# Deriving the second norm's statistics from the first's, and casting six first parts on ScalarE

## The chip, the cores and the metric

The kernel runs on one core of one Trainium2 chip. The metric is the device time of one execution in microseconds. Three runs of the kernel before took 723.16, 723.86 and 724.17 us; the median is 723.86.

## What is computed

The input x has 4 batches of 512 tokens with 128 channels. The reference, cut to what matters here:

```python
xn = _layernorm(x)                      # (x - m) / sqrt(v + 1e-5)
x = x + attn0(xn) + block(xn)           # block: h = _ln(xn, g1, b1); causal attention on h;
                                        # a = o @ Wo + bo + xn; h2 = _ln(a, g2, b2); top-2 experts
xn = _layernorm(x)
x = x + attn1(xn) + moe(xn)             # full attention, 8 experts, top 2
```

`attn0` and the attention in `block` are causal, `attn1` is not; each has 16 heads of 8 channels. `block` begins with a second norm of what is normed already. With mean m and variance v of x, the normed xn has mean 0 and variance v/(v + e), so its norm is (x - m) times (v(1 + e) + e²) to the power of -1/2, with e = 1e-5.

## The kernel before, in words

The tokens of a batch lie as 4 tiles of 128 tokens. "u" counts three attentions: 0 is `attn0`, 1 is the one in `block`, 2 is `attn1`. The twelve pairs (batch, u) are worked through in the order of `ATTENTIONS` (line 48). Each attention has 4 quads of 4 heads, and for each quad TensorE computes the scores twice: once for the row maxima ("max", line 896, which VectorE reduces at line 548) and once, transposed, for the exponentials ("scores", line 923, which ScalarE evaluates at line 791). GpSimd zeroes the part above the diagonal (line 1093), and TensorE multiplies by the values (line 944).

Queries and keys are fp32, but the scores' products run in bf16. Therefore each is split into three bf16 parts. A projection ("project", line 864) leaves queries (k = 0) or keys (k = 1) in a PSUM bank. VectorE casts them to the first part (line 499, or line 495 with a bias for u = 1) and subtracts it from the bank to get the remainder (lines 513 and 508). ScalarE casts the remainder to the second part ("second", line 772), GpSimd subtracts for the third ("parts", line 1062). DMAs then lay the parts into a stack for the products (`fill_piece`, line 385). For the first two attentions ScalarE and GpSimd issue a part of these DMAs themselves, SyncE issues all others. The maxima are split likewise by GpSimd, transposed by TensorE, copied to maxT by VectorE (line 558) and laid into the stack by a DMA (line 1217), for which the scores of the quad wait.

A norm is made of three steps. "stats": VectorE takes BN_STATS of the 4 tiles (line 442), aggregates (line 446) and adds epsilon (line 449). GpSimd raises the result to the power of -1/2 (line 1054). "norm": VectorE subtracts and multiplies (line 461). "turn": TensorE transposes the result. The four norms of a batch are x, h (of the normed x), a and y; x and h share one set of small buffers, a and y the other.

The order is written out by hand as a string of letters (`SCORE`, line 101): each letter is the next step of one chain of steps, and the digit behind it is the PSUM bank that the step takes (a digit names the first of two banks where a step takes two; there are 7 banks to take). `plan` (line 125) turns the string into one list of 1363 steps, and every engine walks through that list and does its own share of each step in that order. So an engine that waits in one step holds up all its later steps. `Order` (line 163) works out from the list which step used a bank before and which count of a semaphore stands for it. The chain "A" (`front`) has the norms and projections of a batch; in batches whose second attention comes first (1, 2 and 3), the steps of u = 1 stand before those of u = 0. VectorE, ScalarE and GpSimd each have one counting semaphore for most results (`vector_done`, `scalar_done`, `gpsimd_done`).

The parts that the change and the prediction touch are the "stats" and "norm" steps of h and x, the "project" steps of VectorE, the steps "second" and "scores" of ScalarE, and the "norm" step of GpSimd (line 1051).

## Time and profile before

| what | value |
|---|---|
| median of three runs | 723.86 us |
| the profiled execution | 722.89 us |
| its span, first to last instruction | 721.1 us |
| mean granted TensorE clock | 0.985 |
| TensorE busy | 686.5 us (95%) |
| VectorE busy | 571.8 us (79%), 1127 instructions |
| ScalarE busy | 527.9 us (73%), 645 instructions |
| GpSimd busy | 194.1 us (27%), 461 instructions |
| VectorE's row maxima, line 548 | 344.5 us in 320 instructions |
| ScalarE's exponentials, line 791 | 288.2 us in 320 instructions |

TensorE is busy for nearly the whole span, so most of what the other engines do is hidden beside it. What counts is where TensorE stands idle, and what it waits for there.

### The profile page before, as it was taken

How to read it: one execution, taken by the hardware profiler on the slowest of the kernel's cores; microseconds unless marked ns; L12 is line 12 of the kernel's file. 1: busy time of each engine (PE TensorE's matmuls, PEld its weight loads, DVE VectorE, ACT ScalarE, POOL GpSimd, SP SyncE). 2: the span in 40 equal slices, each digit the busy share in tenths (PEclk: the TensorE clock that was granted, in tenths of full speed). 3: DMA queues.
4: the chain of work that ended last, by engine and by line, in shares of the span. 5: the costliest groups of instructions: out<-in, count | busy, mean ns of one | idle time of the engine just before them, and what ended most of it. 6: DMA issues, size and time to landing. Idle time of an engine off the chain costs nothing.

```text
span 721.1 us, 27651 instructions
## 1 busy us (share of the span) xinstructions
PE 686.5 (95%) x12078; PEld 344.1 (48%) x12078; DVE 571.8 (79%) x1127; ACT 527.9 (73%) x645; POOL 194.1 (27%) x461
## 2 busy tenths in 40 slices
PE   5688999999999999999999999999999999999996
PEld 2333344665744545544444246556454565533234
DVE  5899999365696888889999777766887667699965
ACT  7167777777777687877879976786878556787892
POOL 5165546112341111313543000123362001020010
PEclk9599999999999999999999999999999999999999
DMA  6140464201130120113132200030040000030001
GB/s 155 36 106 16 125 200 127 72 5 65 36 89 13 34 80 3 36 36 87 52 102 71 63 5 22 4 107 13 23 133 17 4 5 21 28 91 13 28 26 41
DMA packets 42151, 39.52 MB, mean 55 GB/s; under 512 B 14360, under 2 KB 37328, under 8 KB 41808
## 3 DMA queue, kind: packets, MB, share of 16 engines
q1 hardware_dynamic: 40688, 36.20, 17.8%
q8 instruction: 95, 1.56, 0.9%
q10 hardware_dynamic: 1152, 1.05, 0.6%
q0 software_dynamic: 192, 0.52, 0.3%
q14 instruction: 24, 0.20, 0.1%
HBM read 10.47 MB, written 1.44 MB: 17 GB/s over the span
## 4 chain that ended last, share of the span: by engine, by line
PE 78%; DVE 10%; ACT 5%; DMA 2%; issue 2%; SPq 2%; POOL 1%; ACTq 0%; POOLq 0%; DVEq 0%
PE psum L845 44%; PE psum L944 15%; PE psum L923 9%; PE psum L896 8%; DVE neg_max L548 6%; ACT probs L791 2%; SPq L395 2%; PE psum L901 1%; ACT k_stack L729 1%; DMA q_stack<-part 1%; PE psum L861 1%; ACT probs L815 1%; DVE acc L703 1%; DMA heads_inv<-inverses 1%; DMA q_stack<-maxT 1%
## 5 line engine op out<-in xcount | busy, mean ns | idle before, releaser
L548 DVE TENSOR_REDUCE neg_max<-psum 128x2 f32<-128x1024 f32 (+2 forms) x320 | 344.5, 1111 | 57.4 <-PE psum L901 31.1
L791 ACT ACTIVATE probs<-psum 128x1024 f32<-128x1024 f32 (+1 forms) x320 | 288.2, 939 | 108.2 <-PE psum L923 106.2
L944 PE MATMUL psum<-probs,v_ones 128*32 128x512 f32 (+3 forms) x1536 | 158.0, 494 | 0.0
L815 ACT ACTIVATE probs<-psum,col 128x512 f32<-128x512 f32 x160 | 100.8, 686 | 57.7 <-PE psum L845 57.3
L896 PE MATMUL psum<-k_stack,q_stack 64*128 64x512 bf16 (+3 forms) x768 | 114.9, 333 | 17.1 <-DMA q_stack<-part 9.3
L1093 POOL TENSOR_SCALAR_AFFINE_SELECT probs<-probs 128x512 f32<-128x512 f32 x128 | 81.0, 639 | 177.0 <-ACT probs L791 161.5
L845 PE MATMUL psum<-ew,probs 128*32 128x128 f32 x4096 | 124.4, 274 | 0.0
L845 PEld LDWEIGHTS psum<-ew,probs 128*32 128x32 f32 x4096 | 109.7, 110 | 18.8 <-issue 17.1
L845 PE MATMUL psum<-normed_T_a,ew 128*32 128x512 f32 x1024 | 117.1, 593 | 0.8 <-DVE neg_max L548 0.7
L923 PE MATMUL psum<-q_stack,k_stack 64*128 64x512 bf16 (+3 forms) x768 | 110.7, 329 | 5.2 <-DVE neg_max L548 2.4
L743 ACT ACT_TABLE_LOAD x76 | 97.5, 1283 | 1.3
L703 DVE SCALAR_TENSOR_TENSOR acc<-psum,gate,acc 128x128 f32<-128x128 f32 x256 | 72.0, 343 | 19.7 <-PE psum L845 18.0
L1079 POOL CAST max_part<-neg_max 128x16 bf16<-128x16 f32 x48 | 9.5, 198 | 250.8 <-DVE neg_max L548 249.2
L896 PEld LDWEIGHTS psum<-k_stack,q_stack 64*128 64x128 bf16 x768 | 36.9, 95 | 83.8 <-issue 27.8
L923 PEld LDWEIGHTS psum<-q_stack,k_stack 64*128 64x128 bf16 x768 | 32.0, 94 | 80.7 <-issue 26.2
L845 PEld LDWEIGHTS psum<-normed_T_a,ew 128*32 128x32 f32 x1024 | 33.3, 110 | 58.2 <-issue 50.3
L944 PEld LDWEIGHTS psum<-probs,v_ones 128*32 128x32 f32 x1536 | 36.4, 108 | 41.9 <-issue 31.2
L901 PEld LDWEIGHTS psum<-above,pick 64*128 64x128 bf16 x1024 | 45.9, 97 | 16.4 <-issue 1.4
L901 PE MATMUL psum<-above,pick 64*128 64x64 bf16 x1024 | 52.9, 194 | 0.0
L845 PE MATMUL psum<-wout,probs 128*32 128x128 f32 x1024 | 33.7, 275 | 0.1
L1062 POOL TENSOR_TENSOR part<-rest,part 128x512 bf16<-128x512 f32 x24 | 27.7, 1172 | 13.4 <-ACT part L772 13.4
L845 PEld LDWEIGHTS psum<-wout,probs 128*32 128x32 f32 x1024 | 26.7, 110 | 8.4 <-issue 5.2
(132 smaller groups left out, 476.7 us busy)
## 6 DMA issues: line engine op xcount, KB each, us to landing
q_stack<-part SPq DMA_DIRECT2D x66, 128.0 KB, 2.5
k_stack<-part SPq DMA_DIRECT2D x66, 128.0 KB, 2.5
heads_raw<-head_sums SPq DMA_DIRECT2D x24, 128.0 KB
heads_inv<-inverses SPq DMA_DIRECT2D x12, 256.0 KB, 3.4
ew<-w_expert_in SPq DMA_DIRECT2D x4, 512.0 KB, 4.5
ew<-w_expert_out SPq DMA_DIRECT2D x4, 512.0 KB, 5.4
q_stack<-k_stack SPq DMA_DIRECT2D x14, 128.0 KB, 2.3
q_stack<-maxT SPq DMA_DIRECT2D x48, 32.0 KB, 1.9
```

What stands on the lines that cost most here:

```text
L548: eng.tensor_reduce(neg_max[:, q % 2, :, xs[0]:xs[-1] + 1, i], src, AX_X, ALU.max, negate=True).then_inc(vector_done.sem, 1)
L703: eng.scalar_tensor_tensor(out=acc_of[b % 2][:, t, :], in0=src[:, t * P:(t + 1) * P], scalar=gate_of[layer][:, t, expert:expert + 1], in1= ...
L743: eng.preload_act_table(table)
L791: eng.activation(dst, src, ACT.Exp, scale=SCALE).then_inc(probs_ready.sem, 1)
L815: ins = eng.activation(probs[:, order.slot[step[:-1]], 2 * k + f, :], two_banks(step)[:, f, :], ACT.Gelu_apprx_tanh if layer else ACT.Gelu ...
L845: ins = eng.matmul(dst[some, :], kept[:, some], moving, start=start, stop=stop)
L896: ins = eng.matmul(dst[:, a, col0:col0 + keys], q_stack[slot][rows_of, head, i * P:(i + 1) * P], k_stack[slot][rows_of, head, 0:keys], sta ...
L901: ins = eng.matmul(dst[:, a, col0:col0 + HALF], pick[rows_of, upper, :], above[rows_of, upper, :], start=False, stop=upper == 1)
L923: ins = eng.matmul(dst[:, a, n * width:(n + 1) * width], k_stack[slot][rows_of, head, j * P:(j + 1) * P], q_stack[slot][rows_of, head, TIL ...
L944: ins = eng.matmul(sum_bank[32 * c:32 * c + V_COLS, q0:TILES * P], v_ones[u][:, j, g // 2 * QH + c, col0:col0 + V_COLS], probs[:, order.sl ...
L1062: eng.tensor_tensor(part[:, k, 2, :], rest[:, k, :], part[:, k, 1, :], ALU.subtract).then_inc(gpsimd_done.sem, 1)
L1093: eng.affine_select(out=diagonal, in_=diagonal, compare_op=ALU.is_ge, fill=no_chance, base=0, pattern=[[0, QH], [1, P]], channel_multiplie ...
```

## The change

1. The step "stats" of h is dropped (4 of 1363 steps, one for each batch). In "stats" of x VectorE makes two values from the same variance: v + e for the first norm, and v(1 + e) + e² for the second. GpSimd's pow then takes both at once, 8 columns instead of 4, and the pow for h is dropped. The norm of h reads x and its mean instead of the normed x, and the second half of the pow's result.
2. For three attentions, (batch 0, u = 1), (batch 1, u = 1) and (batch 1, u = 0), the first parts of queries and keys are cast by ScalarE, at the place of the "project" step in its own order: an ACTIVATE of Identity with a bias for u = 1, of Copy for u = 0. VectorE waits for it and then subtracts as before.
3. The next batch's x may be loaded only when the norm of h has been made too, and GpSimd's pow of x waits for the norm of h of the batch before.
4. The order of the remaining 1359 steps is the same, but 543 of the 920 steps that take a bank have another bank number. Most of that is a renaming: in 36 steps the step that used the bank before is another one than it was.

The diff, without the string of the order:

```diff
+CAST_BY_SCALAR = ((0, 1), (1, 1), (1, 0))
...
-                  ("second", b, 0, 1), ("parts", b, 0), ("stats", b, "h"), ("norm", b, "h"), ("project", b, 0, 2),
+                  ("second", b, 0, 1), ("parts", b, 0), ("norm", b, "h"), ("project", b, 0, 2),
...
-            if kind in ("second", "gate_exp") or kind == "values" and step[3] % 2 == 1 and step[4] == TILES - 1 or \
+            if kind in ("second", "gate_exp") or kind == "project" and step[3] < 2 and step[1:3] in CAST_BY_SCALAR or kind == "values" and step[3] % 2 == 1 and step[4] == TILES - 1 or \
...
-            if kind in ("norm", "bias", "parts"):
+            if kind in ("bias", "parts") or kind == "norm" and step[2] != "h":
...
-        minus_half = sb("minus_half", [P, TILES])
+        minus_half = sb("minus_half", [P, 2, TILES])
...
-        var_eps_of = [sb(f"var_eps{n}", [P, TILES]) for n in range(2)]
-        rstd_of = [sb(f"rstd{n}", [P, TILES]) for n in range(2)]
+        var_eps_of = [sb(f"var_eps{n}", [P, 2 - n, TILES]) for n in range(2)]
+        rstd_of = [sb(f"rstd{n}", [P, 2 - n, TILES]) for n in range(2)]
...
+            if part_of == 0 and (b, u) in CAST_BY_SCALAR:
+                return scalar_done.sem, order.act["project", b, u, side]
...
-                    eng.tensor_scalar(var_eps[:, :], mean_var[:, :, 1], EPS, None, ALU.add)\
+                    if what == "x":
+                        eng.tensor_scalar(var_eps[:, 1, :], mean_var[:, :, 1], 1.0 + EPS, EPS * EPS, ALU.mult, ALU.add)\
+                           .then_inc(vector_done.sem, 1)
+                        vector_done.count()
+                    eng.tensor_scalar(var_eps[:, 0, :], mean_var[:, :, 1], EPS, None, ALU.add)\
                        .then_inc(vector_done.sem, 1)
...
-                    src = {"x": x_in, "h": normed["x"], "a": a_sum, "y": acc_of[b % 2]}[what]
+                    src = {"x": x_in, "h": x_in, "a": a_sum, "y": acc_of[b % 2]}[what]
...
-                    eng.wait_ge(gpsimd_done.sem, order.pool[step])
+                    eng.wait_ge(gpsimd_done.sem, order.pool["norm", b, "x" if what == "h" else what])
                     for t in range(TILES):
                         eng.tensor_scalar(normed[what][:, t, :], src[:, t, :], mean_var_of[n_set][:, t, 0:1],
-                                          rstd_of[n_set][:, t:t + 1], ALU.subtract, ALU.mult)\
+                                          rstd_of[n_set][:, int(what == "h"), t:t + 1], ALU.subtract, ALU.mult)\
                            .then_inc(vector_done.sem, 1)
...
-                    if u == 1:
-                        eng.tensor_scalar(part[:, k, 0, :], src, bias_qk[:, k:k + 1], None, ALU.add)\
-                           .then_inc(vector_done.sem, 1)
-                        n = vector_done.count()
+                    if (b, u) in CAST_BY_SCALAR:
+                        eng.wait_ge(scalar_done.sem, order.act[step])
                     else:
...
+                if kind == "project" and step in order.act:
+                    u, k = step[2:]
+                    part = part_of_attention(b, u)
+                    eng.wait_ge(work_full.sem, order.work[step] + 1)
+                    if u == 1:
+                        eng.activation(part[:, k, 0, :], one_bank(step), ACT.Identity, bias=bias_qk[:, k:k + 1])\
+                           .then_inc(scalar_done.sem, 1)
+                    else:
+                        eng.activation(part[:, k, 0, :], one_bank(step), ACT.Copy).then_inc(scalar_done.sem, 1)
+                    assert scalar_done.count() == order.act[step]
+                elif kind == "second":
...
-                elif kind == "norm":
+                elif kind == "norm" and step[2] != "h":
...
-                    eng.tensor_tensor(rstd_of[n_set][:, :], var_eps_of[n_set][:, :], minus_half[:, :], ALU.pow)\
+                    if n_set == 0 and b > 0:
+                        eng.wait_ge(vector_done.sem, order.dve["norm", b - 1, "h"])
+                    eng.tensor_tensor(rstd_of[n_set][:, :, :], var_eps_of[n_set][:, :, :], minus_half[:, 0:2 - n_set, :], ALU.pow)\
                        .then_inc(gpsimd_done.sem, 1)
...
-                        eng.wait_ge(vector_done.sem, order.dve["norm", b - 1, "x"])
+                        eng.wait_ge(vector_done.sem, max(order.dve["norm", b - 1, "x"], order.dve["norm", b - 1, "h"]))
```

## Rows read from the trace of the kernel before

**Rows 1.** Busy time by stretch; columns: stretch, length, PE, PEld, DVE, ACT, POOL, clock, DMA

```profile
21.00:60.00 39.00, 32.17 (x446) 14.95 (x442) 36.64 (x52) 18.55 (x25) 16.75 (x42) 0.80 0.23 59
60.00:130.00 70.00, 65.60 (x1004) 28.91 (x1002) 64.11 (x111) 50.87 (x65) 37.92 (x77) 1.00 0.41 120
130.00:330.00 200.00, 198.95 (x3955) 111.53 (x3948) 150.22 (x327) 150.41 (x177) 44.08 (x102) 1.00 0.16 46
```

**Rows 2.** Groups by line, busy us and mean ns; the first from one tile's view

```profile
L442 DVE BATCH_NORM_STATS2 stats<-normed_x x16: 271/275/284, 13.1 to 305.6; 128x6 f32<-128x128 f32 x16
...
L1054 POOL TENSOR_TENSOR rstd<-var_eps,minus_half 128x4 f32<-128x4 f32 x16 | 16.3, 1018 | 36.1 <-DVE var_eps L449 27.2 <-PE psum L845 8.7
...
L1081 POOL TENSOR_TENSOR max_rest<-neg_max,max_part 128x16 f32<-128x16 f32 x48 | 10.5, 219 | 4.0
...
L495 DVE TENSOR_SCALAR part<-psum,bias_qk 128x512 bf16<-128x512 f32 x8 | 6.0, 745 | 1.6 <-PE psum L845 1.6
...
L815 ACT ACTIVATE probs<-psum,col 128x512 f32<-128x512 f32 x160 | 100.8, 686 | 57.7 <-PE psum L845 57.3
...
L799 ACT ACTIVATE head_sums<-psum 128x512 f32<-128x512 f32 x24 | 14.4, 600 | 7.7 <-PE psum L944 7.6
...
L743 ACT ACT_TABLE_LOAD x76 | 97.5, 1283 | 1.3
```

**Rows 3.** Timeline of the start; start us, us, engine, idle before and releaser in brackets

```profile
6.50 1.14 DVE L461 TENSOR_SCALAR normed_x<-x_in,mean_var,rstd 128x128 f32<-128x128 f32 x4 [1.21 <-POOL rstd L1054]
...
8.39 3.60 ACT L729 ACTIVATE k_stack<-one_row 128x4096 bf16<-128x4096 bf16 x1
...
11.13 0.69 DVE L513 TENSOR_TENSOR rest<-psum,part 128x512 f32<-128x512 f32 x1
...
20.81 0.29 PE L896 MATMUL psum<-k_stack,q_stack 64*128 64x128 bf16 x2 [8.32 <-DMA q_stack<-part]
```

**Rows 4.** Timeline at the norms of batch 1

```profile
60.23 1.04 POOL L1054 TENSOR_TENSOR rstd<-var_eps,minus_half 128x4 f32<-128x4 f32 x1
...
61.46 1.76 DVE L461 TENSOR_SCALAR normed_x<-x_in,mean_var,rstd 128x128 f32<-128x128 f32 x4
...
64.01 0.86 DVE L442 BATCH_NORM_STATS2 stats<-normed_x 128x6 f32<-128x128 f32 x4
...
65.40 0.29 DVE L558 CAST maxT<-psum 128x128 bf16<-128x128 f32 x1
...
64.15 0.39 PE L896 MATMUL psum<-k_stack,q_stack 64*128 64x512 bf16 x2 [0.46 <-DVE neg_max L548]
...
69.38 0.39 PE L923 MATMUL psum<-q_stack,k_stack 64*128 64x512 bf16 x2 [1.01 <-DMA q_stack<-maxT]
```

**Rows 5.** Timeline at the projections of batch 0, u = 1

```profile
36.02 1.72 ACT L791 ACTIVATE probs<-psum 128x1024 f32<-128x1024 f32 x2 [1.39 <-PE psum L923]
...
38.51 0.75 DVE L508 SCALAR_TENSOR_TENSOR rest<-psum,bias_qk,part 128x512 f32<-128x512 f32 x1
```

**Rows 6.** Timeline at the projections of batch 1, u = 1

```profile
72.22 1.06 PE L845 MATMUL psum<-normed_T_h,proj_qk 128*32 128x512 f32 x8
...
73.66 1.51 ACT L791 ACTIVATE probs<-psum 128x768 f32<-128x768 f32 x2 [1.09 <-PE psum L923]
...
75.61 0.75 DVE L508 SCALAR_TENSOR_TENSOR rest<-psum,bias_qk,part 128x512 f32<-128x512 f32 x1
...
77.37 0.39 PE L923 MATMUL psum<-q_stack,k_stack 64*128 64x512 bf16 x2 [0.42 <-DVE neg_max L548]
```

**Rows 7.** Timeline at the projections of batch 1, u = 0

```profile
109.29 1.94 ACT L791 ACTIVATE probs<-psum 128x1024 f32<-128x1024 f32 x2 [0.72 <-PE psum L923]
...
111.19 0.69 DVE L513 TENSOR_TENSOR rest<-psum,part 128x512 f32<-128x512 f32 x1
...
112.60 0.68 DVE L570 TENSOR_TENSOR headsT<-heads_raw,heads_inv 128x512 f32<-128x512 f32 x1
...
113.55 1.08 PE L845 MATMUL psum<-projs,headsT 128*32 128x128 f32 x32
```

More of the change, by code:

```diff
@@ L117 @@
[L117 to L121 removed]
+AAAAAAAA6A6A0AAKAAKA1KM2M4M0M2M4M0M2M4M0T6M2A4M0M2M4S0A6S2S0A4S2KM0T6M2AS4VAAM0M2VS4M0KAVM2M4M0S2A6M4S2M0AKM2VS4T6M0
@@ new lines @@
+S4AM2S4M0AVS2M4M0S2AM4VT6S2VS0AS4VM2M0M4AS2VS0S2M4S0VT6S2M4AS0VS2VVS0M4HM2VS0A6M4S2VVM0HT6A2S4S0A6KAM4S2AKAVM0S2S4M2
+VM0S4HVKS2M0VS4M2S0T6M4M2VS0M4VM2S0M4S2M0VHHT6S4M2VM0S4HS2VM4LS0S2VM0M4S2H6S0M2S4LVVT6M0S2M4LHVS0M2VM4M0VVM2HS4A6S0T
+4M2S4A6S0HM2S4VM0S4A6S2HS4A0VHT6S2AM4VAAHA1S2S4H6VS2KFM0S4FVS2VS4VVS2M0S4F6KVM2M0AM4F6E2E0E4E2FVKFVO6AAS0M4M2OE0T2E4
+E2O6S0M4LM2OS4S0AVE2HAO6M4M0S2OE4VT6M2M0M4VE2O6M0S4M2OS0M4M2VE0E4E2T6F4E0O6M4LS2M0OM4M2E0VO6M4M2S0OS4F2HM0HO3T6AE4OO
+6S0HS4S2OS0HS4M2VVS0FA6M2FS4S0VVVS4M2S0F6HVS4M2S0F6F4FFFF5KH0FA6KS2S4A1VVFKI2AI4VAF6S0M2M4VF6G2AE0T6A3A6M4HM0FM2VFA6
@@ L122 @@
+2OE0E4T6M2M0O6M4M2M0OE4E2O6T2M0S4M2OVGS4M0M2O6S4M0M2OVHS4M0S2VE4VGE2E0HHO6HE4HOO4S2S0F6HOH6FM2S0I4T6I0FVF6S2M4S0VF6S
+4F2S0S4KFJ6VFFKM0M2S4J6S0S4VM2S0VS4M2S0J6S4KM2VM0S4VT6S2M4S0J6S2S4M0VHM2S0M4VS2M0G6S4VS2M0S4J6M2S0VM4S0T6VM2S0M4J6S2
+S0VM4S2VM0S4M2VS0M4VM2S0HF6S4M0S2M4VS0M2HI4M0I2T6M4M0VS2M4J6HS0M2S4VS0M4HT6VS2M0S4VHS2M0G6S4VS2M0S4J6S2M0VS4M2VM0S4H
+6S2S0S4VT6VS2GS0G6GGVS4S2S0J6VS4S2VS0S4VS2G6VJ4HVG6I0I2HHHJ6J0J1J6HJ0HJ1H6G
 """
@@ L434, in _ @@
                     what = step[2]
-                    src = {"x": x_in, "h": normed["x"], "a": a_sum, "y": acc_of[b % 2]}[what]
+                    src = {"x": x_in, "a": a_sum, "y": acc_of[b % 2]}[what]
                     n_set = "xhay".index(what) // 2
@@ L439, in _ @@
                         eng.wait_ge(x_loaded, 16 * (b + 1))
-                    after_writer({"x": "var_eps0", "h": "normed_x", "a": "a_sum", "y": f"acc{b % 2}"}[what], f"var_eps{n_set}")
+                    after_writer({"x": "var_eps0", "a": "a_sum", "y": f"acc{b % 2}"}[what], f"var_eps{n_set}")
                     for t in range(TILES):
@@ L453, in _ @@
                     what = step[2]
-                    src = {"x": x_in, "h": normed["x"], "a": a_sum, "y": acc_of[b % 2]}[what]
+                    src = {"x": x_in, "h": x_in, "a": a_sum, "y": acc_of[b % 2]}[what]
                     n_set = "xhay".index(what) // 2
@@ L493, in _ @@
                     part = part_of_attention(b, u)
-                    if u == 1:
-                        eng.tensor_scalar(part[:, k, 0, :], src, bias_qk[:, k:k + 1], None, ALU.add)\
-                           .then_inc(vector_done.sem, 1)
-                        n = vector_done.count()
-                    else:
-                        eng.tensor_copy(part[:, k, 0, :], src).then_inc(vector_done.sem, 1)
-                        n = vector_done.count()
-                    order.dve["part", b, u, k] = n
-                    eng.wait_ge(vector_done.sem, n)
+                    if (b, u) in CAST_BY_SCALAR:
+                        eng.wait_ge(scalar_done.sem, order.act[step])
+                    else:
+                        if u == 1:
+                            eng.tensor_scalar(part[:, k, 0, :], src, bias_qk[:, k:k + 1], None, ALU.add)\
+                               .then_inc(vector_done.sem, 1)
+                            n = vector_done.count()
+                        else:
+                            eng.tensor_copy(part[:, k, 0, :], src).then_inc(vector_done.sem, 1)
+                            n = vector_done.count()
+                        order.dve["part", b, u, k] = n
+                        eng.wait_ge(vector_done.sem, n)
                     p = order.projects.index((b, u))
```

37 lines of the change are left out of this document (14 added, 23 removed).

## The prediction

> **What bounds the kernel now.** The span cut at the places where its character changes comes first [rows 1]. TensorE is busy 32.17 of the 39 us from 21 to 60 and 65.60 of the 70 from 60 to 130. Between 130 and 330 us it is busy 198.95 of 200. So an edit can pay or cost at the start and in these two early stretches, and from 130 us on VectorE has room (150.22 of 200) that nobody waits for. In 21 to 60 us and 60 to 130 us VectorE itself is nearly full (36.64 of 39, 64.11 of 70): work taken off it there may count, and so may every wait put into its queue.
>
> Then the prices of the operations [rows 2], then the stretches of the timeline in which the edits lie: the start [rows 3], the norms of batch 1 [rows 4], the second layer's projections of batch 0 [rows 5], batch 1's second layer [rows 6] and batch 1's first layer [rows 7]. In those the reader is to see which engine ends the others' idle time, in brackets.
>
> Everything is counted against the profiled execution, 722.89 us (span 721.1 and 1.8 around it). The median of the three runs is 723.86, so I add my sum to the median.
>
> **Part 1, the statistics of the second norm.** Per batch this removes four BN_STATS, four aggregations, one small add and one pow, and adds one small multiply-add to the first norm's statistics; the pow of the first norm becomes eight columns wide instead of four. The removed VectorE work of batches 2 and 3 lies past 130 us (the last of its 16 BN_STATS starts at 305.6 [rows 2]), in the stretch where TensorE hardly ever waits [rows 1]: worth nothing. The added small operation and the wider pow there are covered by the same stretch, and if that cover were gone they would cost under 1 us a batch. The load of the next x waits for one norm more; that norm is over long before the bias additions for which the load waits already: nothing.
>
> The wide pow is the unknown. A four-column pow takes 1018 ns on GpSimd, a subtraction of sixteen columns 219 ns [rows 2]. So some 0.8 us of the pow is the function itself. If that is a fixed charge, eight columns cost 1.0 us; if it goes by column, 1.0 + 0.8 = 1.8 us. I take 1.8: a subtraction with four times the columns costs a fifth of the pow, so the charge looks tied to the elements computed.
>
> Batch 0. VectorE waits 1.21 us for that pow before the first normalisation [rows 3]. Adding 0.8 for the pow and 0.1 for the extra small operation moves the projections by 0.9. The remainder of k=0 is made from 11.13 to 11.82, and ScalarE, which has to make its second part, is clearing keys until 8.39 + 3.60 = 11.99 [rows 3]: 0.1 to 0.2 of slack. The other parts follow, through ScalarE, GpSimd and the DMAs, up to the first products at 20.81, for which TensorE has waited 8.32 us [rows 3]. Cost between 0 (narrow pow, or a later issue of the DMAs absorbed by those still under way) and 0.8; I take **+0.7**, since no row shows a place that absorbs it. The statistics and the second pow removed in batch 0 are no gain: VectorE waits for those same products afterwards.
>
> Batch 1. VectorE's first normalisation starts at 61.46, right behind the pow that ends at 60.23 + 1.04 = 61.27 [rows 4]. A pow of 1.8 us ends at 62.1, so with the small addition the normalisation and the maximum behind it are 0.8 later. TensorE, which waits 0.46 for that maximum at 64.15, waits 0.8 longer. Against that the statistics from 64.01 to the copy of maxT at 65.40 disappear: 1.39 us [rows 4]. That copy starts the DMA that TensorE waits for at 69.38. But TensorE idles only 1.01 us there. With both edits it arrives at 68.37 + 0.8 = 69.17 and the DMA lands at 69.33 - 1.39 + 0.8 = 68.74, so TensorE goes on at 69.17: **-0.2**. With a narrow pow it would be -0.9.
>
> **Part 2, six casts on ScalarE.** VectorE needs 745 ns for a cast with bias [rows 2] and 0.69 us for a pass without [rows 3]. On ScalarE the nearest rows are the gelu of 512 columns with a bias column, 686, and the copy of the sum bank, 600. So the operation is no dearer. The Trainium skill ("ScalarE: Activation LUTs", Rules for kernel authors) says to leave add and copy-like work to VectorE; by that rule each cast would be the slower one, but for these fp32 operands in PSUM the rows say the reverse. What decides is the queue. ScalarE takes the cast in the order of the plan, behind the exponentials that stand before it, and VectorE's subtraction now waits for it with the maxima queued behind.
>
> Batch 0, layer 1: the first cast finds ScalarE idle and costs what it did. Behind it two exponentials run from 36.02 to 37.74 [rows 5]. They move by 0.1, the second cast runs 37.8 to 38.5, and the subtraction starts at 38.55 instead of 38.51: **0**. ScalarE is then 0.5 late, but it has waited 1.39 us for TensorE before those exponentials and is far from full in this stretch (18.55 of 39 us [rows 1]).
>
> Batch 1, layer 1: TensorE ends the first projection at 72.22 + 1.06 = 73.28. ScalarE was idle until 73.66 and did two exponentials, 1.51 us [rows 6]. Now: cast 73.35 to 74.05, exponentials to 75.5, second cast to 76.2, and the second subtraction starts at 76.2, not 75.61. So VectorE wins nothing on the first and is 0.6 late after the second. The maximum behind it is what TensorE waits 0.42 for at 77.37 [rows 6]: **+0.6**.
>
> Batch 1, layer 0: ScalarE stood idle for 0.72 us before two exponentials of 1.94 us that started at 109.29 [rows 7]. The first cast fills that gap to 109.5, the exponentials end at 111.4, and the second cast ends at 112.05. The second subtraction began at 111.19 [rows 7]: 0.9 late. Next are the copy of maxT, a maximum and headsT (112.60 to 113.28), and the output projection on TensorE starts at 113.55 with no idle time; 0.3 of slack, so **+0.6**. The statistics of a and its normalisations hang on that projection.
>
> The second parts on ScalarE and the thirds on GpSimd move 0.5 to 1 us with this. They feed stacks that are read later; I price that at nothing, and at 0.3 each (three layers) in the upper bound, should the cover be thinner.
>
> **Part 3, the banks.** The steps keep their order, but 36 of some 900 steps that take a bank follow another user, nearly all in pairs that have changed places. Eight of these lie before 130 us. The waits of TensorE before a maximum or a score are 0.2 to 1.0 us each [rows 4, 6], in either direction: 0, with bounds of 0.5.
>
> **Sum:** 0.7 - 0.2 + 0 + 0.6 + 0.6 + 0 = +1.7 us. 722.89 becomes 724.6, the median 723.86 becomes 725.5. Some 0.2% (1.45 us) is what a measurement of this kernel can tell from no change, and the sum stands just above it.
>
> **Rivals.**
> *The pow costs little for eight columns.* Then the start costs 0.1 and batch 1's norms bring 0.9, and the sum is 0.1 - 0.9 + 0.6 + 0.6 = +0.4: 724.3, no change. For it: nothing in the trace shows a pow of another width. Against it: 0.8 us is much for a fixed charge where GpSimd's other small operations cost 0.2.
>
> *The casts are really gone from VectorE's queue (the other side).* It decides at the second cast of each pair. If ScalarE has its two exponentials behind it when the projection ends, the cast overlaps VectorE's own queue and no wait is left. Then TensorE's 0.42 at 77.37 goes, layer 0 gives 0.3 and layer 1 of batch 0 up to 0.8 (a cast of 0.75). With the narrow pow: 0.1 - 0.9 - 0.4 - 0.3 - 0.8 = -2.3: 721.6, faster. Against it: in both places of batch 1 the exponentials start after the first projection has ended [rows 6, 7], so ScalarE can't be ahead.
>
> *The cast's function is not among those loaded.* The rows know only copies and gelu beside the exponentials. A reload before each of the four biased casts and back again would be eight loads of 1.28 us [rows 2], about half of them on the chain: +5 on top, 730.5, and 10 at most. The Trainium skill ("ScalarE: Activation LUTs", Table sets: the hidden batching unit) says that identity and copy are in every set; by that the count of loads stays 76. I give this 0.04.
>
> *The clock at the start.* From 21 to 60 us TensorE is granted 0.80 of its clock in the mean [rows 1], which is some 16 us at the lower level (1.2 GHz), after TensorE had sat idle until 20.8. If the shifted start makes it rise earlier or later against the work, a tenth of those 16 us, 1.6, may come or go. This widens the range only.
>
> **How the numbers follow.** Forecast as summed 0.45, narrow pow 0.30, casts gone from the queue 0.13, reload 0.04, and 0.08 for delays of ScalarE and GpSimd reaching TensorE after all (+3.5: 727.4). The forecast's own spread of 1 us puts seven tenths of it above 725.3; of the narrow pow one tenth is above and one tenth below 722.4. Slower: 0.32 + 0.03 + 0.04 + 0.08 = 0.47. Faster: 0.11 + 0.03 = 0.14. Within 0.2%: 0.39. The range goes from 722.3, which leaves out most of the faster rival, to 727.7, which takes in the late delays and leaves out the reload.
>
> **What would show it.** The pow of eight columns near 1.8 us; VectorE's wait for it at the start near 2.0; the first products near 21.5; no idle time of TensorE before the scores at 69; VectorE idle before the second subtraction of each pair, released by ScalarE, 0.6 to 1.2 us long; TensorE's busy time unchanged, with its idle time before 130 us up by 1.7; from 130 us on all steps shifted alike. A pow near 1.0, second subtractions without a wait, or TensorE idle in a new place after 130 us would make the forecast wrong.

## The result, and the profile after

The changed kernel takes 726.98 us (median of 7 runs, 724.93 to 727.93), the kernel before 723.51 (7 runs, 721.68 to 724.17): a ratio of 1.0047, 95% interval 1.0032 to 1.0061. It is slower by 3.4 us. The forecast was 725.5 with a range of 722.3 to 727.7, so the sign and the range hold, and the sum of +1.7 is half of what was measured. The profiled execution after took 726.37 us (span 724.6), 3.5 over the one before.

The same stretches as [rows 1], of the changed kernel (columns as there):

```profile
21.00:60.00 39.00, 30.57 (x392) 14.01 (x392) 32.82 (x41) 17.09 (x24) 15.43 (x39) 0.76 0.22 58
60.00:130.00 70.00, 64.90 (x1018) 28.73 (x1020) 62.42 (x108) 53.10 (x68) 37.35 (x75) 1.00 0.41 120
130.00:330.00 200.00, 199.07 (x3924) 111.17 (x3917) 144.78 (x298) 149.77 (x178) 44.66 (x105) 1.00 0.15 43
```

From 130 us on TensorE is as full as before: VectorE has lost 5.4 us of work there, and nobody gains by it. Between 21 and 60 us TensorE is busy 1.6 us less than before and VectorE 3.8 less, although the two casts taken off VectorE there are only 1.5 of it; work has moved out of this window because the engines waited in it. All of the loss is before 119 us. TensorE's busy time over the whole span isn't unchanged, as was forecast: it rose from 686.5 to 688.7 us, at a mean granted clock of 0.980 instead of 0.985. So some 2.2 of the 3.5 us lie in TensorE's longer busy time, and the rest is idle time.

The timeline of the start, against [rows 3]:

```profile
5.52 1.65 POOL L1076 TENSOR_TENSOR rstd<-var_eps,minus_half 128x8 f32<-128x8 f32 x1 [0.98 <-DVE var_eps L456]
...
7.21 1.13 DVE L468 TENSOR_SCALAR normed_x<-x_in,mean_var,rstd 128x128 f32<-128x128 f32 x4 [1.84 <-POOL rstd L1076]
...
8.48 0.63 PE L881 MATMUL psum<-ident,normed_x 128*128 128x128 f32 x4 [1.75 <-DVE normed_x L468]
...
9.99 3.26 PE L865 MATMUL psum<-normed_T_x,proj_qk 128*32 128x512 f32 x16 [0.88 <-DVE normed_T_x L486]
...
11.98 0.69 DVE L509 CAST part<-psum 128x512 bf16<-128x512 f32 x1 [2.14 <-PE psum L865]
```

The wide pow takes 1.65 us where the narrow one takes 1.02 [rows 2], and VectorE waits 1.84 us for it. The row not looked for is the fourth: the first projections take 3.26 us, before the change 1.92. TensorE had been idle for 1.75 us ahead of the transposes. In the microsecond from 9 to 10 us its granted clock is 0.66 on average, and from 10 to 12 it is at the lower of its two levels (1.2 instead of 2.4 GHz).

At 57 us, the place of the first two steps whose banks changed places:

```profile
54.48 1.47 ACT L764 ACTIVATE v_ones<-ident 128x1536 f32<-128x1536 f32 x1
55.99 0.37 ACT L769 ACTIVATE v_ones<-minus_half 128x32 f32<-128x32 f32 x2
56.24 0.58 ACT L811 ACTIVATE probs<-psum 128x512 f32<-128x512 f32 x1
...
56.96 0.51 PE L943 MATMUL psum<-q_stack,k_stack 64*128 64x512 bf16 x2 [1.64 <-ACT probs L811]
...
57.94 1.51 PE L964 MATMUL psum<-probs,v_ones 128*32 128x384 f32 x8
...
57.00:58.00 1.00, 1.00 (x12) 0.51 (x16) 0.17 (x1) 0.43 (x1) 0.52 (x1) 0.55 0.00 0
58.00:59.00 1.00, 1.00 (x9) 0.30 (x12) 0.96 (x1) 0.59 (x1) 0.00 (x0) 0.50 0.00 0
```

The scores now take the bank that an exponential frees, and ScalarE has that exponential behind the clearing of a v_ones (54.48 to 56.4). TensorE waits 1.64 us. Then the clock is at the lower level for some 3.4 us, and the values take 1.51 us instead of the 0.85 that they take in f_pair, where the clock didn't fall there.

Batch 1, against [rows 4], [rows 6] and [rows 7]:

```profile
63.43 1.67 POOL L1076 TENSOR_TENSOR rstd<-var_eps,minus_half 128x8 f32<-128x8 f32 x1
...
67.68 0.28 DVE L568 CAST maxT<-psum 128x128 bf16<-128x128 f32 x1
...
75.94 0.69 ACT L784 ACTIVATE part<-psum,bias_qk 128x512 bf16<-128x512 f32 x1 [0.78 <-PE psum L865]
76.53 1.50 ACT L811 ACTIVATE probs<-psum 128x768 f32<-128x768 f32 x2
77.91 0.70 ACT L784 ACTIVATE part<-psum,bias_qk 128x512 bf16<-128x512 f32 x1
...
78.70 0.75 DVE L518 SCALAR_TENSOR_TENSOR rest<-psum,bias_qk,part 128x512 f32<-128x512 f32 x1 [1.23 <-ACT part L784]
...
114.68 0.69 DVE L523 TENSOR_TENSOR rest<-psum,part 128x512 f32<-128x512 f32 x1 [1.63 <-ACT part L787]
...
116.08 1.51 DVE L580 TENSOR_TENSOR headsT<-heads_raw,heads_inv 128x512 f32<-128x512 f32 x1
...
115.89 2.73 POOL L1084 TENSOR_TENSOR part<-rest,part 128x512 bf16<-128x512 f32 x2 [1.08 <-ACT part L792]
...
117.65 1.08 PE L865 MATMUL psum<-projs,headsT 128*32 128x128 f32 x32 [1.03 <-DVE headsT L580]
```

Cast, two exponentials, cast: ScalarE does them in the order foreseen, and VectorE waits 1.23 and 1.63 us before the second subtractions. The last three rows are new. headsT took 0.68 before [rows 7], with GpSimd's parts starting 0.29 after it:

```profile
112.89 2.54 POOL L1062 TENSOR_TENSOR part<-rest,part 128x512 bf16<-128x512 f32 x2 [0.95 <-ACT part L772]
```

Now the parts start 0.19 ahead of it, it takes 1.51, and TensorE's output projection, which had no idle time before it [rows 7], waits 1.03 us for it.

### The profile page after: what moved, and what is told of

Same layout as the page of the kernel before. It is cut to its first block, busy times and chain, and to the rows that moved or that the text cites. A ratio compares the mean times of both kernels' runs of the same rounds, so it can differ in the third digit from the quotient of the medians.

```text
span 724.6 us, 27619 instructions
## 1 busy us (share of the span) xinstructions
PE 688.7 (95%) x12078; PEld 344.7 (48%) x12078; DVE 563.5 (78%) x1089; ACT 531.1 (73%) x651; POOL 193.4 (27%) x457
## 3 DMA queue, kind: packets, MB, share of 16 engines
q8 instruction: 95, 1.56, 0.9%
## 4 chain that ended last, share of the span: by engine, by line
PE 79%; DVE 12%; ACT 4%; issue 2%; DMA 1%; POOL 1%; ACTq 0%; SPq 0%; DVEq 0%; POOLq 0%
PE psum L865 44%; PE psum L964 15%; PE psum L943 9%; PE psum L916 8%; DVE neg_max L558 7%; ACT probs L811 3%; PE psum L921 1%; DVE acc L713 1%; PE psum L881 1%; ACT probs L835 1%; DVE headsT L580 1%; DMA heads_inv<-inverses 1%; POOL rstd L1076 0%; ACT L753 0%; DMA q_stack<-part 0%
## 5 line engine op out<-in xcount | busy, mean ns | idle before, releaser
L865 PEld LDWEIGHTS psum<-ew,probs 128*32 128x32 f32 x4096 | 109.7, 110 | 18.7 <-issue 17.1
L943 PEld LDWEIGHTS psum<-q_stack,k_stack 64*128 64x128 bf16 x768 | 31.9, 94 | 81.1 <-issue 28.2
L865 PE MATMUL psum<-normed_T_y,win 128*32 128x512 f32 x256 | 29.8, 595 | 1.1 <-DVE rest L518 1.1
```

Source lines behind the costliest of these rows:

```text
L865: ins = eng.matmul(dst[some, :], kept[:, some], moving, start=start, stop=stop)
L943: ins = eng.matmul(dst[:, a, n * width:(n + 1) * width], k_stack[slot][rows_of, head, j * P:(j + 1) * P], q_stack[slot][rows_of, head, TIL ...
```

## Where the 3.5 us are: one table

VectorE's own landmarks cut the span: its first maximum, the first BN_STATS of batch 1, three copies of maxT (73.19, 82.70 and 104.14 in the kernel before), the a_sum (114.77) and the end (721.1). In the profiled execution before, the pieces are 21.46, 35.85, 15.88, 9.51, 21.44, 10.63 and 606.33 us. The table has what each kernel's profiled execution adds to each. The kernels are those of the next section.

| kernel | to 21 | 21-57 | norms, 57-73 | casts, 73-83 | 83-104 | casts, 104-115 | rest |
|---|---|---|---|---|---|---|---|
| after | +0.67 | +1.82 | +0.03 | +0.92 | -0.70 | +1.35 | -0.59 |
| e_old_banks | +1.24 | +1.92 | -0.86 | +0.92 | -0.70 | +1.35 | -0.47 |
| e_stats_only | +1.16 | +1.56 | -0.86 | +0.06 | -0.69 | 0.00 | +0.87 |
| e_casts_only | -0.16 | +0.83 | +0.01 | +0.83 | -0.69 | +1.35 | -0.57 |
| e_banks_only | +0.05 | +0.40 | +0.14 | -0.01 | -0.33 | -0.01 | +0.26 |
| f_k0 | +1.00 | +2.47 | -0.56 | +0.33 | -0.68 | +0.12 | +0.52 |
| f_narrow | -0.02 | +1.69 | -0.32 | +0.92 | -0.69 | +1.35 | +0.57 |
| f_pair | +0.11 | +1.27 | -0.70 | +0.92 | -0.69 | +1.35 | +0.14 |
| f_warm | -0.21 | +1.61 | +0.10 | +0.92 | -0.69 | +1.35 | -0.18 |
| g_after_clear | -0.13 | +0.96 | -0.54 | +0.92 | -0.70 | +1.35 | +0.84 |
| g_narrow | -0.01 | +0.10 | -1.14 | +0.07 | -0.34 | -0.01 | +0.03 |
| g_best | +0.03 | +0.52 | -1.14 | +0.08 | -0.64 | 0.00 | +0.35 |
| g_before_clear | -0.24 | -1.47 | +0.01 | 0.00 | -0.32 | +0.06 | +0.86 |

The two columns of the casts repeat to 0.1 us between kernels that share the edit, and the norms to about 0.3 where no fall of the clock lies just ahead of them. The column 83-104 repeats too, at -0.7 to -0.6 in ten kernels and at -0.3 in three, and the forecast had nothing there. VectorE's two waits for TensorE in it, 0.15 and 0.43 us in the kernel before, are 0 and 0.07 in the changed kernel, and the headsT in it takes 1047 ns instead of 1132. Kernels with the casts alone and with the statistics alone both have the -0.7, and no run says why. The piece from 21 to 57 and the rest don't repeat: one execution of one kernel is only good to about 1 us there. Where the clock rises, and whether it falls again, is what differs. In the kernel before it is back at its full level at 37.0 us, in g_before_clear at 31.9, in e_stats_only at 39.0. Between the warm-up matmuls and 130 us TensorE has the lower level for 27.3 us in the changed kernel and for 20.5 in the kernel before. The runs of the kernel before alone reach from 720.8 to 726.4 us. So a verdict needs the ratio of many runs, and the table says where it comes from.

## The experiments

All were timed in 5 rounds beside the kernel before. Its median was 723.46, 722.43 and 723.54 us in the three groups (e, f and g; 35, 23 and 24 runs).

| kernel | median, runs | ratio | 95% interval |
|---|---|---|---|
| e_old_banks | 725.21, 12 | 1.0016 | 1.0003 to 1.0030 |
| e_banks_only | 724.56, 11 | 1.0014 | 1.0001 to 1.0027 |
| e_casts_only | 724.70, 12 | 1.0013 | 1.0004 to 1.0022 |
| e_stats_only | 723.11, 11 | 0.9989 | 0.9977 to 1.0000 |
| f_warm | 725.87, 6 | 1.0039 | 1.0024 to 1.0055 |
| f_narrow | 725.20, 11 | 1.0029 | 1.0016 to 1.0043 |
| f_pair | 725.53, 7 | 1.0042 | 1.0027 to 1.0057 |
| f_k0 | 724.65, 12 | 1.0025 | 1.0010 to 1.0039 |
| g_narrow | 721.70, 6 | 0.9959 | 0.9943 to 0.9974 |
| g_after_clear | 727.24, 8 | 1.0044 | 1.0029 to 1.0058 |
| g_best | 721.76, 11 | 0.9971 | 0.9956 to 0.9985 |
| g_before_clear | 723.58, 12 | 0.9990 | 0.9975 to 1.0004 |

### One part at a time

**e_old_banks**: the changed kernel, each step with its bank of before. Only the digits of `SCORE` differ, here at the places 77 to 100:

```diff
-AVS2M4M0S2AM4VT6S2VS0AS4VM2M0M4AS2VS0S2
+AVS2M4M0S4AM2VT6S0VS4AS2VM0M4M2AS0VS4S0
```

> The changed kernel with the bank numbers of the kernel before. Theory A (three prices that add up: banks 1.4 us, casts 1.4, statistics 0.7): about 2.1 us over the kernel before, some 725.6; TensorE has no idle 1.6 us near 57 us, where the first scores of the third quad wait for an exponential that ScalarE has queued behind its clearing of the value tile, and the granted clock stays at full after 38 us. Theory B (the casts delay ScalarE, and that stall follows from them): the stall stays and the time is 3.4 over the kernel before.

**e_banks_only**: the kernel before with the banks of after, the same edit the other way round.

```diff
-AVS2M4M0S4AM2VT6S0VS4AS2VM0M4M2AS0VS4S0
+AVS2M4M0S2AM4VT6S2VS0AS4VM2M0M4AS2VS0S2
```

> The kernel before with nothing changed but the bank numbers. Theory A: 1.4 us slower than the kernel before (725.0), with the stall of 1.6 us near 55 us. Theory B: no change.

**e_casts_only**: the kernel before with the six casts, and everything else of it kept. The casts' own lines on ScalarE are those of the change.

```diff
+CAST_BY_SCALAR = ((0, 1), (1, 1), (1, 0))
...
+                    if (b, u) in CAST_BY_SCALAR:
+                        eng.wait_ge(scalar_done.sem, order.act[step])
```

> The kernel before with nothing changed but the six casts on ScalarE. Theory A: 1.4 us slower (0 to 0.4 at batch 0's layer, 0.5 at 76 us, 0.6 to 0.8 at 112 us), VectorE's second subtraction of each pair starts 0.5 to 0.9 later. Theory B: 2.8 us slower, with a stall of TensorE near 55 us.

**e_stats_only**: the changed kernel without the casts and with the banks of before (the digits as in e_old_banks).

```diff
-CAST_BY_SCALAR = ((0, 1), (1, 1), (1, 0))
+CAST_BY_SCALAR = ()
```

> The kernel before with nothing changed but the statistics (second norm derived, one pow of eight columns). Theory A: 0.7 us slower (start +0.7, batch 1's norms between -0.2 and 0), pow 1.65 us. Rival (the wide pow is harmless after the start, and the 1.4 us of statistics removed in batch 1 come back in full): 0.3 faster than the kernel before.

By the ratios the banks cost 1.0 us alone, the casts 0.9, and the statistics bring 0.8 (the interval ends at 1.0000). The last was a miss of the expectation, which had 0.7 slower. The statistics and the casts together (e_old_banks) cost 1.2. All three cost 3.4, and the sum of the single ones is 1.1. So the banks, priced at nothing, cost 1.0 alone and 2.2 on top of the others. Each ratio is good to about 1 us to either side, so the 1.0 may be 0.1, and the 2.2, by the two intervals taken together, may be 0.8 or 3.6: that the banks cost something is shown, how much more than alone isn't. The profiled executions don't show it at all: e_old_banks, the slow end of whose runs was profiled (726.25 of 722.46 to 726.71), has +1.92 in the piece 21-57 without the new banks. Their traces show three things.

First, without the casts the subtraction of batch 1 starts with no wait and headsT takes 0.68 again. This is the view of VectorE in e_stats_only:

```profile
77.50 0.75 DVE L518 SCALAR_TENSOR_TENSOR rest<-psum,bias_qk,part 128x512 f32<-128x512 f32 x1
...
112.43 0.69 DVE L523 TENSOR_TENSOR rest<-psum,part 128x512 f32<-128x512 f32 x1
113.03 0.28 DVE L568 CAST maxT<-psum 128x128 bf16<-128x128 f32 x1
113.83 0.68 DVE L580 TENSOR_TENSOR headsT<-heads_raw,heads_inv 128x512 f32<-128x512 f32 x1
```

Second, the start is 1.2 us late in e_old_banks and e_stats_only, and the clock had fallen sooner than after the change: nearly all of the transposes were at the lower level too. TensorE's timeline in e_stats_only:

```profile
1.26 4.96 PE L876 MATMUL psum<-zeros 128*128 128x512 bf16 x14 [1.26 <-DVE zeros L405]
8.49 1.09 PE L881 MATMUL psum<-ident,normed_x 128*128 128x128 f32 x4 [2.27 <-DVE normed_x L468]
```

Third, the wait at 57 us belongs to the banks and the fall of the clock behind it doesn't belong to them alone. With the banks of before the scores there wait 0.55 to 0.61 us in the kernel before, g_before_clear, g_narrow and g_best, and 0.87 or 0.88 with the casts or the wide pow, always for VectorE's maximum. With the banks of after they wait for the exponential, 1.31 us in e_banks_only and 1.57 to 1.65 in the kernels with casts:

```profile
55.72 0.39 PE L923 MATMUL psum<-q_stack,k_stack 64*128 64x512 bf16 x2 [1.31 <-ACT probs L791]
```

But in e_old_banks and e_stats_only, with the banks of before, the clock fell too, at 53 us, where none had been expected. The granted clock in e_old_banks (columns as in [rows 1]):

```profile
53.00:56.00 3.00, 2.82 (x30) 1.30 (x30) 2.87 (x5) 1.89 (x3) 2.59 (x8) 0.51 0.21 60
```

And with the banks of after it fell behind the wait in three executions (after, f_warm, f_narrow) and held in three (e_banks_only, f_k0, g_after_clear).

### The start: a wider pow, or the clock behind it

**f_warm**: the changed kernel with more warm-up matmuls, so that TensorE is idle for 0.69 us instead of 1.75.

```diff
-EARLY = 14
+EARLY = 21
```

> The changed kernel with 21 instead of 14 warm-up matmuls ahead of the first transposes. In the changed kernel TensorE sat idle for 1.75 us before those transposes (0.87 before the change), its granted clock fell at 9 to 10 us and the first two projections took 3.26 us instead of 1.92. Theory A (the wide pow costs more than its own 0.7 us, because the longer wait also lets the clock fall): the idle time goes, the projections take 1.9 to 2.0 again, VectorE's first remainder starts 1.3 us earlier, the first products come 0.3 to 0.7 us earlier, and the time falls by 0.5 to 1 us against the changed kernel, to 1.0033 to 1.0041 of the kernel before. Theory B (the DMAs absorb whatever the start loses, so the clock there is worth nothing): the projections are as quick, but the first products stay within 0.2 us and the ratio stays at 1.0047. If the extra matmuls themselves come late, the transposes start after 8.6 us and the ratio is above 1.005.

**f_narrow**: the changed kernel with two narrow pows. The part on VectorE's side, which waits for the second pow before the norm of h, is left out here.

```diff
...
-                elif kind == "norm" and step[2] != "h":
+                elif kind == "norm":
...
-                    eng.tensor_tensor(rstd_of[n_set][:, :, :], var_eps_of[n_set][:, :, :], minus_half[:, 0:2 - n_set, :], ALU.pow)\
+                    row = int(step[2] == "h")
+                    eng.tensor_tensor(rstd_of[n_set][:, row, :], var_eps_of[n_set][:, row, :], minus_half[:, 0, :], ALU.pow)\
```

> The changed kernel with two pows of four columns in place of one of eight: the first norm's pow as before the change, the derived one issued by GpSimd at its old place, with its operand long there. Casts and banks are the changed kernel's. Theory A (the wide pow is the dear part of the derived statistics): the first pow takes 1.02, VectorE waits 1.2 for it, the first products come 0.7 us or more earlier than in the changed kernel, batch 1's first normalisation starts at most 0.2 late instead of 1.2, and the time falls by 1 to 2.5 us: ratio 1.0013 to 1.0033. Theory B (what was lost is lost at the casts and the banks, and the pow's width is absorbed by the DMAs): within 0.5 us of the changed kernel, ratio 1.004 to 1.005.

TensorE's start in f_warm:

```profile
1.26 6.53 PE L876 MATMUL psum<-zeros 128*128 128x512 bf16 x21 [1.26 <-DVE zeros L405]
8.48 0.63 PE L881 MATMUL psum<-ident,normed_x 128*128 128x128 f32 x4 [0.69 <-DVE normed_x L468]
9.98 1.92 PE L865 MATMUL psum<-normed_T_x,proj_qk 128*32 128x512 f32 x16 [0.88 <-DVE normed_T_x L486]
...
20.61 0.29 PE L916 MATMUL psum<-k_stack,q_stack 64*128 64x128 bf16 x2 [7.83 <-DMA q_stack<-part]
```

The projections take 1.92 again, the parts are still 0.7 us late, and yet the first products are not late at all (20.61; 20.81 in [rows 3]). The last DMA that these products wait for is issued by GpSimd 0.74 us later than in the kernel before and lands no later (20.47 against 20.68). Its issue in the kernel before, then in f_warm:

```profile
17.08 0.53 POOL L395 DMA_DIRECT2D q_stack<-part  x1
...
17.82 0.53 POOL L398 DMA_DIRECT2D q_stack<-part  x1
```

f_pair and g_after_clear say the same: they have the wide pow and 14 warm-ups, their clock happened to hold, and their first maximum is +0.11 and -0.13. The four executions with the wide pow whose clock fell (after, e_old_banks, e_stats_only, f_k0) have +0.67 to +1.24. There this DMA is issued at 18.7 to 19.2 us. So the DMAs absorb the pow's own 0.7 us, and what the start costs is the fall of the clock, in some executions and not in others. In the seven executions with a narrow pow first (of before, e_banks_only, e_casts_only, f_narrow, g_narrow, g_best and g_before_clear), where the transposes start at 7.8 instead of 8.5 us, it never fell. The ratio of f_warm (1.0039) is within the noise of the changed kernel's, so what the kept clock is worth over many runs isn't shown.

The Trainium skill ("TensorE: Matmul & The Clock Gate", Part 1: The HAM clock gate) has the clock depend on how busy TensorE has been. The traces agree as far as they go: after idle times of 0.69 to 1.73 us ahead of the transposes the clock held (f_warm and the seven), after 1.75 to 2.42 it fell four times in six. But the two that held there had the longest idle times, 2.38 and 2.42 us (f_pair, g_after_clear), so the length of the wait doesn't decide it alone.

The narrow pow in the changed kernel gives 1.0029 instead of 1.0047, 1.3 us, which is about what the two columns "to 21" and "norms" say (0.69 + 0.35), though the two intervals overlap.

### The casts: the first or the second of each pair

**f_k0**: only the casts of k = 0 on ScalarE. The same condition stands in two more places, which are left out.

```diff
-                    if (b, u) in CAST_BY_SCALAR:
+                    if k == 0 and (b, u) in CAST_BY_SCALAR:
                         eng.wait_ge(scalar_done.sem, order.act[step])
```

> The changed kernel with only the first cast of each pair on ScalarE; the casts of k=1 stay with VectorE. The prediction has the cost in the second cast, which ScalarE reaches behind its exponentials. Theory A: the subtractions of k=1 start without a wait for ScalarE, VectorE loses nothing in front of the maxima of batch 1, and the time falls by 0.8 to 1.6 us against the changed kernel: ratio 1.0025 to 1.0036. Theory B (VectorE is the fuller engine, so a cast given back costs its 0.7 us each, as much as the wait): within 0.5 us, ratio 1.004 to 1.0054. The subtraction at 112 us may still meet GpSimd's: headsT takes 0.7 if it doesn't, 1.5 if it does.

The ratio falls to 1.0025, 1.6 us, with overlapping intervals. The columns of the casts say the same and repeat: +0.92 and +1.35 become +0.33 and +0.12, 1.8 us less. VectorE in f_k0:

```profile
78.55 0.75 DVE L518 SCALAR_TENSOR_TENSOR rest<-psum,bias_qk,part 128x512 f32<-128x512 f32 x1
...
113.75 0.69 DVE L523 TENSOR_TENSOR rest<-psum,part 128x512 f32<-128x512 f32 x1
...
115.15 0.68 DVE L580 TENSOR_TENSOR headsT<-heads_raw,heads_inv 128x512 f32<-128x512 f32 x1
```

The second casts are most of the cost of the casts, as forecast. The first ones bring nothing (+0.33 and +0.12 are left), even though they take 0.7 us each off the fuller engine: VectorE waits for ScalarE instead.

### The banks: the first pair of steps

**f_pair**: in the changed kernel the scores of layer 0, group 2, and the last maximum of layer 1's group 0 take the banks of their former users again, and with them two more scores, four steps in all; everything else keeps the users of after.

```diff
-AVS2M4M0S2AM4VT6S2VS0AS4VM2M0M4AS2VS0S2
+AVS2M4M0S4AM2VT6S0VS4AS2VM0M4M2AS0VS4S0
```

Behind place 100 the digits are those of after with 0, 2 and 4 renamed to fit.

> The changed kernel with its banks, except that the first pair of steps that had changed places (the scores of layer 0, group 2, tile 0 and the last maximum of layer 1's group 0, at 52 to 57 us) take the banks of before; all other steps follow the same users as in the changed kernel. Theory A (the price of the banks is this one pair: the scores wait for a bank whose exponential stands behind the clearing of v_ones on ScalarE, 1.64 us): the wait falls to 0.6 to 0.9, the clock doesn't dip at 57 to 60, and the time falls by 1 to 1.5 us, to a ratio of 1.0026 to 1.0035. Theory B (the pair only moves a wait that another takes over, since with the first users restored for all banks a wait of 0.88 stood there too): 0 to 0.5 us, ratio 1.004 to 1.0047.

TensorE at that place in f_pair, and its clock behind it:

```profile
56.16 0.39 PE L943 MATMUL psum<-q_stack,k_stack 64*128 64x512 bf16 x2 [0.87 <-DVE neg_max L558]
...
57.23 0.85 PE L964 MATMUL psum<-probs,v_ones 128*32 128x384 f32 x8
...
57.00:58.00 1.00, 1.00 (x18) 0.37 (x14) 0.81 (x2) 0.71 (x1) 0.50 (x1) 1.00 0.00 0
```

The wait is 0.87 us, for VectorE, not 1.64, for ScalarE, and the clock holds. But the ratio (1.0042) can't be told from 1.0047. So what the pair costs in time isn't shown, and which of the 36 steps the price of the banks lies in stays open.

The trace does show one way in which banks and statistics add up to more than their sum. With the fall of the clock behind the pair the norms' column is +0.03 (after) and +0.10 (f_warm); with the same banks and no fall -0.54 and -0.56 (g_after_clear, f_k0); with the old pair -0.70 (f_pair) and -0.86 (e_old_banks and e_stats_only, whose fall is over by 56.5 us). So half a microsecond or more of what the statistics bring is lost in the stretch at the lower level.

**g_after_clear**: the clearing moved to 20 us, where ScalarE has nothing to do.

```diff
-                  ("turn", b, "h"), ("project", b, 1, 0), ("project", b, 1, 1), ("second", b, 1, 0),
+                  ("turn", b, "h")] + ([("clear_v", b, 1)] if b == 0 else [])
+        front += [("project", b, 1, 0), ("project", b, 1, 1), ("second", b, 1, 0),
...
-        front += [("clear_v", b, 1)] if b == 0 else []
```

> The changed kernel with one step moved: ScalarE clears layer 1's v_ones (1.47 + 0.6 us) right behind its sorting of heads, at about 20 us, where it has nothing to do, instead of at 55 us between two exponentials. Theory A (the price of the banks and of everything that comes late at 55 to 60 us is ScalarE's queue there: an exponential stands behind this clearing): TensorE's wait of 1.64 us before the scores at 57 falls below 0.8, no lower clock from 57 to 60, 1 to 2 us gained: ratio 1.0019 to 1.0033. Theory B (the maximum before it on VectorE is what TensorE waits for anyway): 0.5 us or less, ratio 1.004 to 1.0047.

This is a miss of the experiment, not of the theory. The clearing of layer 1 stood at 45 us; the one at 54.5 is that of the third attention (u = 2), and it stayed. Its trace has `v_ones` cleared at 53.62 and the wait unchanged:

```profile
56.10 0.39 PE L943 MATMUL psum<-q_stack,k_stack 64*128 64x512 bf16 x2 [1.64 <-ACT probs L811]
```

So it says that the clearing at 45 us was hidden (1.0044), and whether the pair would cost nothing with the other one gone was not tried. As this clock didn't fall at 57, it also says that a wait of 1.64 us isn't always followed by a fall of the clock.

**g_before_clear**: the same move in the kernel before.

```diff
+                  ("turn", b, "h")] + ([("clear_v", b, 1)] if b == 0 else [])
```

> The kernel before with the clearing of v_ones moved to 20 us and nothing else. Theory A: TensorE's wait of 0.61 and VectorE's behind it near 55 us shrink by 0.3 to 0.8 us, ratio 0.9990 to 0.9996. Theory B: it is hidden here, ratio 1.000. Either way the move is worth less here than in the changed kernel, where the scores wait for the exponential right behind the clearing.

0.9990, not told from 1. The profiled execution is 1.1 us shorter, with -1.47 in the piece 21-57, and its clock rose at 31.9 us instead of 37.0.

### A version that beats both

**g_narrow**: the kernel before with the derived statistics as two narrow pows, no casts, the banks of before. It is f_narrow with two edits more:

```diff
-CAST_BY_SCALAR = ((0, 1), (1, 1), (1, 0))
+CAST_BY_SCALAR = ()
...
-AVS2M4M0S2AM4VT6S2VS0AS4VM2M0M4AS2VS0S2
+AVS2M4M0S4AM2VT6S0VS4AS2VM0M4M2AS0VS4S0
```

> The kernel before with the derived statistics alone, as two pows of four columns; no casts on ScalarE, banks as before. Theory A (batch 1 gains what the statistics and the pow stood for, and only the wide pow had taken it back): the start is that of before (first remainder at 11.13, first products at 20.8), batch 1 gains the 1.4 us between its first normalisation and the copy of maxT, less a wait that appears elsewhere: the time is 0.5 to 1.4 us under the kernel before, ratio 0.9980 to 0.9993. Theory B (TensorE has too little idle time there): ratio 0.9995 to 1.0005. The same statistics with the wide pow gave 0.9989.

**g_best**: g_narrow with the clearing of layer 1 moved (as in g_after_clear) and 17 warm-up matmuls.

```diff
-EARLY = 14
+EARLY = 17
```

> A version meant to beat both kernels: the one with two narrow pows and banks as before, no casts on ScalarE, with the clearing of v_ones moved to 20 us and 17 instead of 14 warm-up matmuls. Theory A (each of the three takes away a wait that is on the chain): 1.5 to 2.5 us under the kernel before, ratio 0.9965 to 0.998. Theory B (the statistics alone are what is to be had): ratio 0.9985 to 0.9993.

g_narrow gives 0.9959 (0.9943 to 0.9974), more than either theory had. Its norms:

```profile
60.32 1.04 POOL L1077 TENSOR_TENSOR rstd<-var_eps,minus_half 128x4 f32<-128x4 f32 x1
```

The column of the norms is -1.14, of which 0.28 is the pow's width (e_stats_only has -0.86). Its profiled execution, 721.77 us, is 1.1 under the one before; the ratio says 3.0 and the medians 1.8. The gain is clear of the noise and its size isn't settled (1.9 to 4.1 by the interval). It is also clear of the same statistics with the wide pow, 0.9977 to 1.0000 in e_stats_only. g_best (0.9971) is no better: the two additions are worth nothing that these runs can measure.

## Why the prediction came out as it did

The sign and the range came out right and the sum was half of what was measured. Part of the agreement is luck: the first term was met by another mechanism, and the casts cost 1.1 us more than forecast while a stretch that was priced at nothing (83-104) gave 0.7 back.

**The start, +0.7.** The value was met by luck (+0.67 in one execution) and the mechanism was wrong. "No row shows a place that absorbs it" fails: the DMAs absorb 0.7 us of late parts. What costs is the clock that falls behind the wait ahead of the transposes: with the wide pow the start is +0.67 to +1.24 in the four executions with the fall and -0.21 to +0.11 in the three without it. The rival on the clock looked at the rise after 20 us; the place was at 9.

**The wide pow.** 1.8 us was taken, 1.65 measured. The choice against 1.0 was right: doubling the columns adds 0.63 us. VectorE waited 1.84 us for it, near the 2.0 of the forecast.

**The norms of batch 1, -0.2 (narrow: -0.9).** Measured alone -0.86 (narrow: -1.14). The idle time before the scores at 69 us is gone, as forecast. But TensorE's wait there was taken as the whole slack, and the landmark on VectorE comes sooner by more than that; VectorE is nearly full here (64.11 of 70 us [rows 1]), so the likely reason, argued and not tested, is that its later maxima come sooner. In the changed kernel the fall of the clock takes it back to +0.03.

**Batch 0, layer 1, casts, 0.** Between the two subtractions there are now 2.61 us (36.96 to 39.57), not 2.22: 0.4 us more. The second cast ended at 39.06 us and the subtraction started 0.5 us later; the trace names no releaser for that half microsecond, so its cause stays open. How much of it reaches the sum is lost in the scatter of that piece.

**Batch 1, layer 1, casts, +0.6.** +0.92. The second cast costs 0.6 (0.92 less the 0.33 of f_k0), as worked out; the first, thought free, costs 0.33.

**Batch 1, layer 0, casts, +0.6.** +1.35. The chain was right (subtraction late by 0.8 against the copy of maxT at 104.14 us); the missing term is headsT, +0.83, for which TensorE waits 1.03 us. f_k0, where headsT takes 0.68 again, has +0.12.

**The second and third parts priced at nothing.** They feed no stack too late: from 21 to 130 us the one wait of TensorE for their DMAs is that for the first products. But the thirds are the very operations of GpSimd that headsT collides with, so "nothing" failed by another road.

**The banks, 0 with bounds of 0.5.** 1.0 alone (0.1 to 2.0), 2.2 on top of the rest by the ratios (some 1.4 to either side). With the casts this is the term that left the sum at half: the step that failed is "in either direction: 0". The nearest rows had waits of up to 1.0; what was not looked up is what stands ahead of the new releaser on its engine, here a clearing of 1.47 us, behind which the wait grew from 0.61 us to 1.31 in e_banks_only and 1.64 after the change. That this wait is where the time goes isn't shown: f_pair took it away and gained nothing that could be measured.

**The rivals.** The pow of 1.0 and the reload didn't come: the loads of the activation tables stay at 76. Nor did the casts leave the queue: the second subtractions of batch 1 waited 1.23 and 1.63 us for them. "Delays of ScalarE and GpSimd reaching TensorE after all", with 727.4 and a chance of 0.08, comes nearest to the measured time; of its mechanism the traces show one case, headsT. The chances have one slip: with a spread of 1 us about 725.5, six tenths and not seven lie above 725.3.

## What to carry to other kernels

When a step takes another bank, look at the new predecessor's engine and at what is queued ahead of the instruction that frees it, not at the mean wait. Moving an operation to an engine with idle time gains nothing if that engine takes it in order behind work that starts after its input is ready; the second of a pair pays. If two results are needed at different times, two narrow slow operations can beat one wide one (0.9959 against 0.9989 here). Where an early wait of TensorE grows, look at the granted clock behind it: the clock may be the dearer part, though filling the wait (f_warm) gave no gain that could be measured.

## What was not expected of the hardware

**VectorE and GpSimd on the same memory.** headsT multiplies two operands of SBUF. Started 0.19 us behind GpSimd's subtraction it takes 1.51 us, in the seven kernels with both casts of batch 1's layer 0 on ScalarE (1.50 or 1.51). In the other seven it starts 0.29 us ahead of the subtraction and takes 0.68. The line's own view in the changed kernel, and that of GpSimd's parts in the window:

```profile
L580 DVE TENSOR_TENSOR headsT<-heads_raw,heads_inv x12: 676/682/1509, 94.4 to 719.3; 128x512 f32<-128x512 f32 x12
...
L1084 POOL TENSOR_TENSOR part<-rest,part x2: 1158/1388/1619, 115.9 to 117.0; 128x512 bf16<-128x512 f32 x2
```

The first part ends at about 117.0, and headsT, from 116.08, ends at 117.59: 0.6 us after it. GpSimd's second part takes 1619 ns instead of the 1162 of the kernel before. In the other order it is GpSimd that pays: its first part takes 1414 ns there instead of 1158. The Trainium skill ("SBUF — State Buffer", Who interferes with whom) says that an operation of VectorE with two inputs in SBUF and one of GpSimd that reads it exclude each other for the whole instruction, whichever comes first. The traces agree in both orders, and a shift of half a microsecond between the two engines decides who pays. A collision of 0.45 us was in the kernel before too: its headsT at 91.19 us, 0.05 behind a GpSimd operation of 0.64 us, took 1.13.

```profile
91.14 0.64 POOL L1093 TENSOR_SCALAR_AFFINE_SELECT probs<-probs 128x512 f32<-128x512 f32 x1 [1.94 <-ACT probs L791]
...
91.19 1.13 DVE L570 TENSOR_TENSOR headsT<-heads_raw,heads_inv 128x512 f32<-128x512 f32 x1
```

**A pow on GpSimd goes by its columns.** 1.02 us for 4 columns and 1.65 for 8; from these two widths some 0.4 fixed and 0.16 a column, an estimate.

**ScalarE casts from PSUM as fast as VectorE.** 0.69 to 0.70 us with a bias and 0.60 to 0.62 without for 512 columns; VectorE takes 0.745 and 0.69. The rule that the prediction cites from the Trainium skill names add, not copies, and is given for bf16; for these fp32 banks neither the add nor the copy was slower on ScalarE. The price of an operation was never the question here.
